# Channel norms from batch norm statistics of two interleaved groups, in place of two sums and a square

## The chip, the cores and the metric

The kernel runs on one core of a Trainium2 chip. The metric is the device time of one launch in microseconds (us). A core has a matrix engine (PE, TensorE, which writes to eight PSUM banks of 512 float32 columns), a vector engine (DVE, VectorE), an activation engine (ACT, ScalarE), a general engine (POOL, GpSimd) and a queue engine for transfers (SP). Each works through its own instruction list in order, and they wait for one another by semaphores. All data are float32.

## The reference, cut to what matters

The input `x` is an image of 128 x 128 positions with C = 32 channels. Four layers each do a convolution-like part and a feed-forward part, and each part first normalises every position over its 32 channels, eight times in all:

```python
def _ln_c(v, eps=1e-06):
    m = jnp.mean(v, axis=-1, keepdims=True)
    s = jnp.var(v, axis=-1, keepdims=True)
    return (v - m) / jnp.sqrt(s + eps)
...
    x = x + _L0_conv_ref(_ln_c(x), ...)
    t = _to_tokens(x)
    t = t + _L0_ffn_ref(_ln_t(t), ...)
    x = _from_tokens(t, x)
    ...
    x = x + _L3_conv_ref(_ln_c(x), ...)
    t = _to_tokens(x)
    t = t + _L3_ffn_ref(_ln_t(t), ...)
```

`_ln_t` is the same with eps 1e-05. What follows a norm is: a gated triangle product with a norm of its own on its output (L0, L1, L3), a mixture with pooled tokens (L0's second part), a recurrence over positions with batch statistics (L1's and L2's second part), a scan over rows with a one-dimensional convolution (L2's first part), and a mixture of eight experts (L3's second part).

## The kernel before

The whole image lies in SBUF as 128 partitions by 4096 floats, in one of two layouts, `XR` (x_rows) and `XC` (x_cols). Along a partition there are S = 32 blocks of G = 4 groups of 32 channels. The kernel is written out by hand, engine by engine: a list of stage functions for each, with semaphores between. The stages are named in the code t0, f0, t1, r1, sc, r2, t3 and f3, in the order in which they run (t: triangle product, f: feed-forward, r: recurrence, sc: scan). Each begins with a channel norm, which goes over Q = 8 chunks of four blocks (512 floats per partition, 16 groups). The helpers `ln_dve_step`, `ln_act_step` and `ln_pool_step` write out step u of this pipeline on their engine:

- DVE at step u: sum of chunk u (L279); sum of the squares of chunk u - 2 (L282); mean of chunk u (L286); reciprocal of the deviation of chunk u - 3 (L289); centring of chunk u into `Z` (L292).
- ACT at step u: root of chunk u - 2 (L301); square of chunk u (L309); copy of the transposed chunk u - 4 from PSUM to `ZT` (L318). Behind the last root it loads the table of the function that comes next (L358), where the stage names one.
- POOL at step u: for chunk u - 3 the memset of a ones channel (L330, only in t0, t1, t3 and f3), then the scaling of `Z` by the reciprocal (L333).
- PE: four transposes of a scaled chunk (L386, banks 0 and 1 in turn), then the stage's first matmuls: projections (L506) in the t stages, gate logits (L779) in f0, `Wx` (L1021) in the r stages, routing (L1376) in f3.

What surrounds the norms differs. In f0, sc and r2 nothing else is on DVE. In t0 the weights of the first stage are made among the first two steps. In t1 each of the first four steps follows four additions of f0's output (L945), whose matmuls (L838) use banks 0 to 3. In t3 each step follows an addition of r2's output (L1177). In r1 and f3 the norm is merged into the output part of the triangle stage in front (t1 and t3): a merged step t has, on DVE, gating (L674), reciprocal (L668) and sum of squares (L662) of the output part before step u = t - 5 of the norm, and on POOL a scaling of the gate (L710) and the addition to x (L715) before it:

```python
            for t in range(TRI_LN + LN_STEPS if after else S // 4 + 4):
                if 4 <= t < S // 4 + 4:
                    out_gate(t - 4)
                if 3 <= t < S // 4 + 3:
                    out_inverse(t - 3)
                if 2 <= t < S // 4 + 2:
                    out_sum(t - 2)
                if after:
                    ln_dve_step(dve, after, t - TRI_LN)
```

## Time and profile before

| | before |
|---|---|
| median of 3 runs | 674.55 us (673.01 to 675.37) |
| profiled execution, its own time | 676.27 us |
| its span | 674.5 us |
| TensorE clock granted, mean | 0.844 of full speed |
| PE busy | 486.4 us (72%) |
| DVE busy | 432.7 us (64%) |
| ACT busy | 279.9 us (42%) |
| POOL busy | 258.8 us (38%) |

The profile is one execution of the program. The span is the time from its first to its last instruction; the execution's own time has some 1.8 us more around it. Busy time counts an engine's instructions without the waits between them. A row's number is a start or a duration in us, and L279 is line 279 of the kernel. A window's row gives its bounds, its length, the busy time of PE, PE's weight loads (PEld), DVE, ACT and POOL with the number of instructions of each, the granted clock, the share of DMA and GB/s.

### The profile page before, as it was taken

How to read it: one execution, taken by the hardware profiler on the slowest of the kernel's cores; microseconds unless marked ns; L12 is line 12 of the kernel's file. 1: busy time of each engine (PE TensorE's matmuls, PEld its weight loads, DVE VectorE, ACT ScalarE, POOL GpSimd, SP SyncE). 2: the span in 40 equal slices, each digit the busy share in tenths (PEclk: the TensorE clock that was granted, in tenths of full speed). 3: DMA queues.
4: the chain of work that ended last, by engine and by line, in shares of the span. 5: the costliest groups of instructions: out<-in, count | busy, mean ns of one | idle time of the engine just before them, and what ended most of it. 6: DMA issues, size and time to landing. Idle time of an engine off the chain costs nothing.

```text
span 674.5 us, 7507 instructions
## 1 busy us (share of the span) xinstructions
PE 486.4 (72%) x2599; PEld 359.3 (53%) x2599; DVE 432.7 (64%) x845; ACT 279.9 (42%) x642; POOL 258.8 (38%) x317
## 2 busy tenths in 40 slices
PE   2788853798487674789459983799489855939992
PEld 1457742487344663389439973398246734713330
DVE  6696449532958659810873459601958497399997
ACT  2766435700375444567370006566479445000000
POOL 1793463200267237500060002300259267037774
PEclk9989976866789798889958997989579985579997
DMA  6000000000000000000000000000000000001212
GB/s 199 1 1 1 0 1 0 1 0 1 0 1 0 1 0 1 0 1 1 1 0 1 1 1 2 0 1 1 1 0 1 1 0 1 0 0 16 32 31 47
DMA packets 19572, 5.95 MB, mean 9 GB/s; under 512 B 17068, under 2 KB 19244, under 8 KB 19501
## 3 DMA queue, kind: packets, MB, share of 16 engines
q1 hardware_dynamic: 19534, 5.46, 3.6%
q8 instruction: 22, 0.36, 0.2%
q14 instruction: 16, 0.13, 0.1%
HBM read 3.36 MB, written 2.10 MB: 8 GB/s over the span
## 4 chain that ended last, share of the span: by engine, by line
PE 42%; DVE 41%; issue 6%; ACT 6%; POOL 4%; DMA 1%; DVEq 0%; SPq 0%; POOLq 0%
PE psum L1239 6%; DVE stats L279 5%; DVE gate L1456 5%; DVE ab L645 4%; PE psum L1000 4%; PE psum L999 4%; PE psum L506 4%; PE psum L536 4%; PE psum L545 4%; PE psum L386 4%; DVE stats L282 3%; DVE z L292 3%; DVE tmp L1450 3%; PE psum L1376 2%; DVE stats L286 2%
## 5 line engine op out<-in xcount | busy, mean ns | idle before, releaser
L333 POOL TENSOR_TENSOR z<-z,stats 128x496 f32<-128x496 f32 (+1 forms) x64 | 79.2, 1238 | 179.2 <-DVE stats L289 179.1
L386 PE MATMUL psum<-ident,z 128*128 128x128 f32 x256 | 58.4, 373 | 78.1 <-POOL z L333 75.5
L386 PEld LDWEIGHTS psum<-ident,z 128*128 128x128 f32 x256 | 40.8, 191 | 109.1 <-POOL z L333 75.1
L506 PE MATMUL psum<-wp_L,z_t 64*128 64x320 f32 x384 | 66.1, 479 | 11.9 <-DVE tmp L645 6.4
L1398 PE MATMUL psum<-we,z_t 128*128 128x512 f32 x128 | 64.7, 640 | 13.8 <-DVE tmp L1450 9.4
L309 ACT ACTIVATE squares<-z 128x512 f32<-128x512 f32 x64 | 40.3, 630 | 55.9 <-DVE z L292 55.9
L545 PE MATMUL psum<-wo_L,z_t 128*128 128x256 f32 x192 | 48.1, 395 | 14.6 <-DVE tmp L674 13.8
L506 PEld LDWEIGHTS psum<-wp_L,z_t 64*128 64x128 f32 x384 | 36.2, 197 | 36.6 <-issue 31.0
L1398 PEld LDWEIGHTS psum<-we,z_t 128*128 128x128 f32 x128 | 23.7, 200 | 54.0 <-DVE tmp L1450 30.1
L710 POOL TENSOR_TENSOR gate<-gate,stats 128x512 f32<-128x512 f32 x24 | 25.1, 1046 | 64.2 <-DVE stats L668 64.2
L318 ACT ACTIVATE z_t<-psum 128x512 f32<-128x512 f32 x56 | 39.8, 715 | 23.0 <-PE psum L386 22.5
L1092 ACT ACTIVATE ab<-psum,mv 128x128 f32<-128x128 f32 x112 | 41.1, 367 | 19.2 <-PE psum L1000 8.7
L1000 PE MATMUL psum<-ab,R_vt 128*128 128x128 f32 x224 | 48.4, 299 | 0.0
L1486 POOL TENSOR_TENSOR z<-tmp 128x512 f32<-128x512 f32 x31 | 39.3, 1268 | 22.9 <-DVE tmp L1450 22.9
L545 PEld LDWEIGHTS psum<-wo_L,z_t 128*128 128x128 f32 x192 | 35.4, 194 | 22.0 <-issue 16.4
L999 PE MATMUL psum<-z_t,wbnt 128*128 128x128 f32 x224 | 46.2, 290 | 0.8 <-DVE wbnt L1145 0.8
L282 DVE TENSOR_REDUCE stats<-squares 128x16 f32<-128x512 f32 x64 | 43.3, 677 | 0.0
L330 POOL MEMSET z<- 128x16 f32 x32 | 3.9, 122 | 98.7 <-ACT squares L309 98.7
L1239 PE MATMUL psum<-ab,toep 128*128 128x128 f32 x336 | 39.4, 280 | 2.5 <-POOL ab L1222 1.6
L1239 PEld LDWEIGHTS psum<-ab,toep 128*128 128x128 f32 x336 | 39.1, 195 | 3.1 <-issue 3.1
L645 DVE TENSOR_TENSOR ab<-psum,sig 128x256 f32<-128x256 f32 x64 | 33.4, 605 | 10.3 <-ACT sig L583 10.3
L1450 DVE TENSOR_TENSOR tmp<-psum,ab 128x1024 f32<-128x1024 f32 x32 | 38.8, 1214 | 0.0
(238 smaller groups left out, 1028.2 us busy)
## 6 DMA issues: line engine op xcount, KB each, us to landing
x_rows<-in_x_dram SPq DMA_DIRECT2D x4, 512.0 KB, 7.3
out_dram<-x_cols SPq DMA_DIRECT2D x32, 64.0 KB, 1.9
par<-in_par_dram SPq DMA_DIRECT2D x1, 644.5 KB
w<-in_w_dram SPq DMA_DIRECT2D x1, 264.0 KB
w<-in_w_dram SPq DMA_DIRECT2D x1, 256.0 KB
mask<-in_mask_dram SPq DMA_DIRECT2D x1, 64.0 KB
row<-in_row_dram SPq DMA_DIRECT2D x1, 3.3 KB
w2l<-in_w2l_dram SPq DMA_DIRECT2D x1, 2.0 KB
```

Of the source, the lines that this page charges most:

```text
L282: dve.tensor_reduce(SS[:, before], SQ4[:, SQ * before:SQ * (before + 1)], AX.X, ALU.add)\
L333: pool.tensor_tensor(Z4[:, r, :, 0:last_c], Z4[:, r, :, 0:last_c], rstd, ALU.mult).then_inc(L.s["z"], 1)
L386: m = pe.transpose(bank(b % 2)[:, k * N:(k + 1) * N], block_of(Z)(4 * b + k), ident[:, :])
L506: m = pe.matmul(bank(slot_bank(s) + h, 2 * 5 * C), ZT[rows, s, :], wp[l][rows, :, :], start=True, stop=True)
L545: m = pe.matmul(PSUM[:, (2 + 2 * (b % 3)) * BANK + k * 2 * GC:(2 + 2 * (b % 3)) * BANK + (k + 1) * 2 * GC], ZT[:, 4 * b + k, :], wo[l][:, ...
L645: dve.tensor_tensor(dst, slot(s)[:, :, :, 2 * C:4 * C], sig, ALU.mult).then_inc(L.s["lin"], 1)
L999: return (pe.matmul(o, W["wbnt"][:, :], chunks(ZTIME, off, h), start=True, stop=False), lambda: pe.matmul(o, W["vt"][:, :], chunks(Y, off, ...
L1000: lambda: pe.matmul(o, W["vt"][:, :], chunks(Y, off, h), start=False, stop=True))
L1092: act.activation(chunks(Y, first + k + 1, h), bank(2 * h + k % 2, NS), ACT.Sigmoid, bias=bias).then_inc(L.s[f"step_y{h}"], 1)
L1239: m = pe.matmul(bank(2 + h, ROWS_S * NB), toep[:, b, :, :], scan_rows(SCN[:, :, b:b + NB], off, h), start=(b == 0), stop=(b == 2))
L1398: m = pe.matmul(o, ZT[:, s, :], we[:, e, :, :], start=True, stop=True)
L1450: dve.tensor_tensor(TMP[:, s % 2, :].rearrange("p (e g c) -> p e g c", e=E3, g=G), PSUM[:, o:o + 2 * BANK].rearrange("p (e g c) -> p e g c ...
```

## The change

For each chunk DVE no longer takes a sum and a sum of squares of 512 elements each, and ACT no longer squares. In their place DVE issues eight `bn_stats` of 64 elements each. One reads two neighbouring groups of 32 channels alternately (channel 0 of the first group, channel 0 of the second, channel 1 of the first, ...), so that the statistics of the even elements are those of one group and the statistics of the odd ones those of the other: count, mean and sum of squared deviations of each, six numbers, into the new tile `moments`. The root is taken of the third number, and the mean is the second, so the multiplication by 1/32 (L286) goes as well.

The pipeline is ordered anew. DVE at step u: statistics of chunk u, then reciprocal and centring of chunk u - 1. ACT at step u: root of chunk u, then the copy of chunk u - 2. POOL at step u: chunk u - 1, now behind the centring instead of the square. A norm has 10 steps instead of 12. In the norms with a ones channel the centring leaves that channel out. Lastly, the output matmuls of f0 use banks 2 to 5 instead of 0 to 3, and in front of them PE waits for the weights of three more stages, whose temporary place those banks were.

```diff
         stats = sb("stats", [N, 4, N])
+        moments = sb("moments", [N, Q, SQ * G, 3])
         ident = sb("ident", [N, N])
...
-            "norm": "sum:8 mean:8 centred:8 square:8 sumsq:8 std:8 rstd:8 z:8",
+            "norm": "moments:8 std:8 rstd:8 centred:8 z:8",
...
         def ln_parts():
-            return [stats[:, k, :].rearrange("p (q s g) -> p q s g", q=Q, g=G) for k in range(4)]
+            return [stats[:, k, :].rearrange("p (q s g) -> p q s g", q=Q, g=G) for k in (0, 3)]
+
+        def ln_moment(q, k):
+
+            return moments[:, q, :, k].rearrange("p (s g) -> p s g", g=G)
...
-        LN_STEPS = Q + LAG + 2
+        LN_STEPS = Q + LAG
+
+        def last_channel(L):
+
+            return C - 1 if "one" in L.s else C
 
         def ln_dve_step(dve, L, u):
 
             X4 = by_block(L.src) if L is sc else blocks(L.src).rearrange("p g s c -> p s g c")
-            Z4, SQ4 = by_block(Z), by_block(SQR)
-            SUM, MEAN, SS, RSTD = ln_parts()
-            q, before, first = u, u - LAG, u - LAG - 1
+            Z4 = by_block(Z)
+            STD, RSTD = ln_parts()
+            q, before = u, u - 1
             if 0 <= q < Q:
                 wait_all(dve, L.ready[q])
-                r = slice(SQ * q, SQ * (q + 1))
-                dve.tensor_reduce(SUM[:, q], X4[:, r], AX.X, ALU.add).then_inc(L.s["sum"], 1)
+                for s in range(SQ):
+                    for g in range(0, G, 2):
+                        k = s * G + g
+                        m = dve.bn_stats(moments[:, q, k:k + 2, :].rearrange("p k m -> p (k m)"),
+                                         X4[:, SQ * q + s, g:g + 2, :].rearrange("p g c -> p c g"))
+                m.then_inc(L.s["moments"], 1)
             if 0 <= before < Q:
-                dve.wait_ge(L.s["square"], L.at["square"] + before + 1)
-                dve.tensor_reduce(SS[:, before], SQ4[:, SQ * before:SQ * (before + 1)], AX.X, ALU.add)\
-                    .then_inc(L.s["sumsq"], 1)
+                r, c = slice(SQ * before, SQ * u), last_channel(L)
+                dve.wait_ge(L.s["std"], L.at["std"] + before + 1)
+                dve.reciprocal(RSTD[:, before], STD[:, before]).then_inc(L.s["rstd"], 1)
+                dve.wait_ge(L.s["moments"], L.at["moments"] + before + 1)
+                dve.tensor_tensor(Z4[:, r, :, 0:c], X4[:, r, :, 0:c],
+                                  ln_moment(before, 1).unsqueeze(3).to_broadcast([N, SQ, G, c]), ALU.subtract)\
+                    .then_inc(L.s["centred"], 1)
+
+        def ln_act_step(act, L, u):
+            STD, _ = ln_parts()
+            q = u
             if 0 <= q < Q:
-                dve.wait_ge(L.s["sum"], L.at["sum"] + q + 1)
-                dve.tensor_scalar(MEAN[:, q], SUM[:, q], 1.0 / C, None, ALU.mult).then_inc(L.s["mean"], 1)
-            if 0 <= first < Q:
-                dve.wait_ge(L.s["std"], L.at["std"] + first + 1)
-                dve.reciprocal(RSTD[:, first], SUM[:, first]).then_inc(L.s["rstd"], 1)
-            if 0 <= q < Q:
-                dve.wait_ge(L.s["mean"], L.at["mean"] + q + 1)
-                dve.tensor_tensor(Z4[:, r], X4[:, r], over_c(MEAN[:, q]), ALU.subtract).then_inc(L.s["centred"], 1)
-
-        def ln_act_step(act, L, u):
-            Z4, SQ4 = by_block(Z), by_block(SQR)
-            SUM, _, SS, _ = ln_parts()
-            q = u - LAG
-            if 0 <= q < Q:
-
-                act.wait_ge(L.s["sumsq"], L.at["sumsq"] + q + 1)
-                act.activation(SUM[:, q], SS[:, q], ACT.Sqrt, bias=eps[:, L.eps:L.eps + 1],
+                act.wait_ge(L.s["moments"], L.at["moments"] + q + 1)
+                act.activation(STD[:, q], ln_moment(q, 2), ACT.Sqrt, bias=eps[:, L.eps:L.eps + 1],
                                scale=(1.0 + L.e2) / C).then_inc(L.s["std"], 1)
                 if q == Q - 1 and L.function is not None:
                     warm_table(act, L.function)
-            q = u
-            if 0 <= q < Q:
-                r = slice(SQ * q, SQ * (q + 1))
-                act.wait_ge(L.s["centred"], L.at["centred"] + q + 1)
-                act.activation(SQ4[:, r], Z4[:, r], ACT.Square).then_inc(L.s["square"], 1)
-            q = u - LAG - 2
+            q = u - LAG
             if 0 <= q < Q:
                 act.wait_ge(L.s["zt_ps"], L.at["zt_ps"] + q + 1)
                 dst = ZT[:, 4 * q:4 * q + 4, :]
@@ -318,19 +319,16 @@
                 act.activation(dst, bank(q % 2).rearrange("p (s n) -> p s n", s=4), ACT.Copy).then_inc(L.s["zt"], 1)
 
         def ln_pool_step(pool, L, u):
-            q = u - LAG - 1
+            q = u - 1
             if 0 <= q < Q:
-                Z4, r = by_block(Z), slice(SQ * q, SQ * (q + 1))
-                pool.wait_ge(L.s["square"], L.at["square"] + q + 1)
-                last_c = C
+                Z4, r, c = by_block(Z), slice(SQ * q, SQ * (q + 1)), last_channel(L)
+                pool.wait_ge(L.s["centred"], L.at["centred"] + q + 1)
                 if "one" in L.s:
-
-
-                    last_c = C - 1
-                    pool.memset(Z4[:, r, :, last_c:], 1.0).then_inc(L.s["one"], 1)
+                    pool.memset(Z4[:, r, :, c:], 1.0).then_inc(L.s["one"], 1)
                 pool.wait_ge(L.s["rstd"], L.at["rstd"] + q + 1)
-                rstd = ln_parts()[3][:, q].unsqueeze(3).to_broadcast([N, SQ, G, last_c])
-                pool.tensor_tensor(Z4[:, r, :, 0:last_c], Z4[:, r, :, 0:last_c], rstd, ALU.mult).then_inc(L.s["z"], 1)
+                _, RSTD = ln_parts()
+                pool.tensor_tensor(Z4[:, r, :, 0:c], Z4[:, r, :, 0:c],
+                                   RSTD[:, q].unsqueeze(3).to_broadcast([N, SQ, G, c]), ALU.mult).then_inc(L.s["z"], 1)
 
...
-            for V in (t1, t3):
-                pe.wait_ge(V.s["w_dve"], V.at["w_dve"] + TRI_W)
+            for V, count in ((t1, TRI_W), (t3, TRI_W), (f3, 2), (r1, 1), (r2, 1)):
+                pe.wait_ge(V.s["w_dve"], V.at["w_dve"] + count)
             for b in range(SEGI // 2):
                 if b >= 4:
                     pe.wait_ge(L.s["done"], L.at["done"] + b - 3)
                 for k in range(2):
                     i = 2 * b + k
-                    m = pe.matmul(bank(b % 4)[:, k * SEG * C:(k + 1) * SEG * C], WGT[:, i * N:(i + 1) * N],
+                    m = pe.matmul(bank(2 + b % 4)[:, k * SEG * C:(k + 1) * SEG * C], WGT[:, i * N:(i + 1) * N],
                                   outm[:, :, :], start=True, stop=True)
                 m.then_inc(L.s["y_ps"], 1)
...
                 dve.wait_ge(L.s["y_ps"], L.at["y_ps"] + b + 1)
                 for k in range(2):
                     x = xi[:, 2 * b + k]
-                    i = dve.tensor_tensor(x, x, bank(b % 4)[:, k * SEG * C:(k + 1) * SEG * C]
+                    i = dve.tensor_tensor(x, x, bank(2 + b % 4)[:, k * SEG * C:(k + 1) * SEG * C]
                                           .rearrange("p (s c) -> p s c", s=SEG), ALU.add)
```

**Order, first place.** DVE in the middle of f0's norm, before (`stats` holds sums, means, deviations and reciprocals, `squares` the squares, `z` the centred values):

```order
L279 TENSOR_REDUCE stats<-x_cols 128x16
L282 TENSOR_REDUCE stats<-squares 128x16
L286 TENSOR_SCALAR stats<-stats 128x16
L289 RECIPROCAL stats<-stats 128x16
L292 TENSOR_TENSOR z<-x_cols,stats 128x512
```

and from the start of f0's norm in the changed kernel:

```order
L290 BN_STATS moments<-x_cols 128x6 x16
L296 RECIPROCAL stats<-stats 128x16
L298 TENSOR_TENSOR z<-x_cols,moments 128x512
L290 BN_STATS moments<-x_cols 128x6 x8
L296 RECIPROCAL stats<-stats 128x16
```

Five instructions for each chunk have become ten, eight of them statistics, and the reciprocal and centring of a chunk now stand behind the statistics of the next.

**Order, second place.** DVE in one full step of r1's norm, which is merged with the output part of t1. Before:

```order
L674 TENSOR_TENSOR tmp<-psum,gate 128x512
L668 RECIPROCAL stats<-stats 128x16
L662 TENSOR_REDUCE stats<-squares 128x16
L279 TENSOR_REDUCE stats<-x_cols 128x16
L282 TENSOR_REDUCE stats<-squares 128x16
L286 TENSOR_SCALAR stats<-stats 128x16
L289 RECIPROCAL stats<-stats 128x16
L292 TENSOR_TENSOR z<-x_cols,stats 128x512
```

and in the changed kernel (its L672, L666 and L660 are the first three of these):

```order
L672 TENSOR_TENSOR tmp<-psum,gate 128x512
L666 RECIPROCAL stats<-stats 128x16
L660 TENSOR_REDUCE stats<-squares 128x16
L290 BN_STATS moments<-x_cols 128x6 x8
L296 RECIPROCAL stats<-stats 128x16
L298 TENSOR_TENSOR z<-x_cols,moments 128x512
```

The centring that stands behind a gating is now that of the chunk one step older than before.

**Order, third place.** POOL at the end of r1's norm, before:

```order
L710 TENSOR_TENSOR gate<-gate,stats 128x512
L715 TENSOR_TENSOR x_cols<-x_rows,tmp 128x4x4x32
L333 TENSOR_TENSOR z<-z,stats 128x512
L715 TENSOR_TENSOR x_cols<-x_rows,tmp 128x4x4x32
L333 TENSOR_TENSOR z<-z,stats 128x512 x5
```

and in the changed kernel (its L708, L713 and L330 are the same three):

```order
L708 TENSOR_TENSOR gate<-gate,stats 128x512
L713 TENSOR_TENSOR x_cols<-x_rows,tmp 128x4x4x32
L330 TENSOR_TENSOR z<-z,stats 128x512
L713 TENSOR_TENSOR x_cols<-x_rows,tmp 128x4x4x32
L330 TENSOR_TENSOR z<-z,stats 128x512 x3
```

Two more of the eight scalings stand among the output part's operations, and two fewer behind them.

## Rows read from the trace of the kernel before

**Rows 1.** The chain that ended last, shares of the span by engine.

```profile
PE 42%; DVE 41%; issue 6%; ACT 6%; POOL 4%; DMA 1%; DVEq 0%; SPq 0%; POOLq 0%
```

**Rows 2.** Windows, one for each norm: t0, f0, t1, r1, sc, r2, t3, f3.

```profile
5.27:29.62 24.35, 13.56 (x52) 8.63 (x52) 18.59 (x50) 11.17 (x23) 10.36 (x17) 1.00 0.32 97
104.11:123.61 19.50, 10.48 (x37) 6.20 (x38) 16.85 (x40) 11.44 (x24) 9.80 (x9) 0.65 0.00 0
169.21:193.61 24.40, 15.28 (x63) 10.13 (x61) 21.08 (x52) 11.18 (x23) 10.37 (x16) 0.69 0.00 0
249.59:280.99 31.40, 17.30 (x68) 11.00 (x67) 29.62 (x59) 17.09 (x33) 24.30 (x21) 0.84 0.00 1
332.85:352.69 19.84, 7.70 (x28) 5.01 (x28) 16.84 (x40) 13.36 (x25) 9.80 (x8) 0.54 0.00 0
408.97:428.34 19.37, 9.79 (x33) 5.62 (x34) 18.04 (x43) 12.15 (x22) 9.79 (x8) 0.74 0.00 1
472.50:495.47 22.97, 10.88 (x43) 6.81 (x41) 20.42 (x47) 11.34 (x24) 10.36 (x16) 0.54 0.00 1
539.01:570.84 31.83, 16.13 (x67) 12.20 (x65) 28.63 (x56) 15.29 (x34) 24.87 (x29) 0.72 0.00 1
```

**Rows 3.** Timeline, f0's norm: start us, us, engine, line, operation.

```profile
110.83 1.33 POOL L333 TENSOR_TENSOR z<-z,stats 128x512 f32<-128x512 f32 x1 [14.55 <-DVE stats L289]
...
114.60 0.65 DVE L292 TENSOR_TENSOR z<-x_cols,stats 128x512 f32<-128x512 f32 x1
114.83 1.33 POOL L333 TENSOR_TENSOR z<-z,stats 128x512 f32<-128x512 f32 x1 [0.66 <-DVE stats L289]
...
115.17 0.68 DVE L279 TENSOR_REDUCE stats<-x_cols 128x16 f32<-128x512 f32 x1
115.77 0.67 DVE L282 TENSOR_REDUCE stats<-squares 128x16 f32<-128x512 f32 x1
...
116.44 0.24 DVE L289 RECIPROCAL stats<-stats 128x16 f32<-128x16 f32 x1
116.60 0.65 DVE L292 TENSOR_TENSOR z<-x_cols,stats 128x512 f32<-128x512 f32 x1
...
122.14 1.28 ACT L358 ACT_TABLE_LOAD   x1
```

**Rows 4.** Timeline, r1's merged norm.

```profile
254.07 1.26 POOL L715 TENSOR_TENSOR x_cols<-x_rows,tmp 128x512 f32<-128x512 f32 x1
254.16 1.21 DVE L286 TENSOR_SCALAR stats<-stats 128x16 f32<-128x16 f32 x1
...
269.76 1.64 DVE L292 TENSOR_TENSOR z<-x_cols,stats 128x512 f32<-128x512 f32 x1
```

**Rows 5.** Groups by line: busy us, mean ns of one, idle before.

```profile
L286 DVE TENSOR_SCALAR stats<-stats 128x16 f32<-128x16 f32 x64 | 19.1, 298 | 0.6
L710 POOL TENSOR_TENSOR gate<-gate,stats 128x512 f32<-128x512 f32 x24 | 25.1, 1046 | 64.2 <-DVE stats L668 64.2
L945 DVE TENSOR_TENSOR x_cols<-x_cols,psum 128x256 f32<-128x256 f32 x16 | 5.7, 414 | 3.1 <-PE psum L838 3.1
L1456 DVE TENSOR_REDUCE gate<-z 128x128 f32<-128x512 f32 x31 | 32.1, 1034 | 0.2 <-POOL z L1486 0.2
```

**Rows 6.** Timeline, r1's batch statistics of 512 contiguous PSUM elements, five together.

```profile
279.71 3.02 DVE L1121 BATCH_NORM_STATS2 bns<-psum 128x6 f32<-128x512 f32 x5
```

**Rows 7.** Timeline, the first constants.

```profile
2.75 0.37 DVE L414 TENSOR_REDUCE d<-ident 128x32 f32<-128x128 f32 x1 [2.75 <-POOL gw L409]
3.04 0.28 DVE L415 TENSOR_REDUCE m<-ident 128x4 f32<-128x128 f32 x1
3.23 0.35 DVE L416 TENSOR_REDUCE d<-ident 128x16 f32<-128x128 f32 x1
```

**Rows 8.** Timeline, t0's third chunk, and f3's sixth scaling (chunk 5).

```profile
12.48 0.68 DVE L279 TENSOR_REDUCE stats<-x_rows 128x16 f32<-128x512 f32 x1
...
567.46 1.02 POOL L333 TENSOR_TENSOR z<-z,stats 128x496 f32<-128x496 f32 x1
```

## The prediction

> **What bounds the kernel now.** I read the chain that ended last first: PE has 42% of it and DVE 41%, and every other engine a few per cent [rows 1]. No engine is full over the whole span, so what a change is worth has to be read stage by stage. The change touches the eight channel norms, called here by the names that their stages have in the code: t0, f0, t1, r1, sc, r2, t3, f3. So I next took one window for each norm, from its first sum (L279) to the end of its last scaled chunk (L333). Added up they are 193.7 us of 674.5, and DVE is busy for 170 us of them [rows 2]. The norms are DVE's: in sc, DVE is busy 16.8 of 19.8 us while PE has 7.7.
>
> The timeline of f0's norm shows the repeating step. The centring starts at 114.60, the next chunk's sum at 115.17, the sum of squares of an older one at 115.77, the mean behind it, the reciprocal at 116.44, the next centring at 116.60: a step of 2.00 us with no gap [rows 3]. The reader should look at starts, not at durations: a reduction lasts 0.68 but the next instruction starts 0.6 after it. In starts, the step is sum 0.60, sum of squares and mean together 0.67, reciprocal 0.16, centring 0.57.
>
> There is a second thing to see, a resource that DVE and POOL hold in turn. In r1's norm POOL's addition L715 runs from 254.07 to 255.33, and the tiny mean beside it takes 1.21 us; over 64 of them the mean is 298 ns, 19.1 us in all [rows 4, 5]. The centring, with two SBUF inputs, is held as well: 1.64 us at 269.76, where that of f0 at 114.60 takes 0.65 [rows 3, 4]. It works the other way too: the scaling at 114.83 starts in the middle of a centring and takes 1.33, where one with nothing beside it takes 1.02 (567.46) [rows 3, 8]. Reductions are not held: those of 115.17 and 115.77 run at their 0.68 under that same scaling [rows 3].
>
> **The change part by part.** Removed for each chunk on DVE: sum, sum of squares, mean, in starts 116.44 - 115.17 = 1.27 us, more where the mean was held (19.1 us of means against 64 x 0.17 = 10.9: 8 us of holding, nearly all in r1 and f3). Removed on ACT: one square of 0.63 us, off the limiting engine except as latency. Added on DVE: eight batch norm statistics of 64 elements. Everything hangs on the price of one, which no row shows. The same operation on 512 elements: five in 3.02 us, each some 0.68 long, so (3.02 - 0.68) / 4 = 0.585 from start to start [rows 6]. Two reductions in order split such a slot into its parts: 0.60 for 512 elements (115.17 to 115.77 [rows 3]) and 0.19 for 128 (L415, 3.04 to 3.23 [rows 7]) give 0.41 / 384 = 1.07 ns an element and 0.05 fixed. With 64 elements that is 0.07 + 0.055 = 0.125: the lower bound, 1.0 us for the eight.
>
> But the new reads alternate between two groups, each element far from the last. The rows price this for reductions. At the kernel's start L414 reads 128 elements with a large inner step and its successor starts 0.29 later, against the 0.19 of L415, which reads the same 128 in order [rows 7]. So 0.10 / 128, about 0.75 ns for each element. L1456 reads 512 strided in 1034 ns, against 0.68 us for the 512 read in order [rows 3, 5]: 0.69 ns. For 64 elements that adds 0.045 to 0.05: **0.17 us each, 1.36 for the eight**. I take this one, since its rows share the access pattern. The upper bound is the whole duration with no overlap, fixed 0.15 + 0.11 for strided elements = 0.26.
>
> The Trainium skill speaks against the change here: "SBUF — State Buffer", section "Specifications (TRN2)", gives 16-byte lines, wants at least two hits on a line for full bandwidth, and charges every crossing to a new one. Interleaved, every read crosses. By that rule the eight cost some 1.36 and the sum below holds, 13.9 us saved; without it 1.0, and 28 saved. The trace agrees (0.29 against 0.19), though with four groups and not two.
>
> So DVE's steady step goes from 2.00 to 1.36 + 0.16 + 0.57 = 2.10: as throughput, the change loses 0.1 us a chunk. What it gains is latency. Before, chunk q was scaled three steps after its first sum (sum, centring, ACT square, sum of squares, ACT root, reciprocal). Now it is one step (statistics, ACT root, reciprocal, centring). And the mean's waits for POOL go.
>
> A new wait takes part of it back: the scaling now needs the centring just before it, and both use the held resource. In the steady part this fits (scaling 1.05 under statistics 1.36). At the end, the last centring waits for the scaling of chunk 6 and the last scaling waits for it: 0.05 + 1.05 + 0.66 + 0.05 + 1.05 = 2.9 us behind chunk 6's centring, 3.0 with the memsets of the norms that have a ones channel. Queued behind that centring on DVE is only the next stage's work.
>
> Norm by norm, after against before [rows 2]:
> - sc: 1.36 + 7 x 2.10 + 2.9 = 19.0 against 19.84; with copies behind it, 1.0 saved.
> - r2: 19.0 against 19.37; 0.5.
> - f0: 19.0 against 19.50, but the first chunk is ready at 1.36 + 2.10 + 1.1 = 4.6 instead of 110.83 + 1.33 - 104.11 = 8.05 [rows 3], 3.4 earlier, so PE no longer ends late; and ACT's table load, which stood ahead of the last copies at 122.14 [rows 3], starts near 119.8, before the last chunk. Between 0.5 and 3.4: 2.4.
> - t0: DVE goes on at 12.48 after the weights in both [rows 8]. 12.48 + 6 x 2.10 + 3.0 = 28.1 against 29.62; with the same table load 1.9.
> - t1: three of its steps have four additions of 0.41 each, overlapped 0.35 [rows 5], so 3.5 a step: 1.36 + 3 x 3.5 + 4 x 2.10 + 3.0 = 23.3 against 24.40; with the load 1.5.
> - t3: six steps have an addition of 512 elements, a slot of 0.60: 1.36 + 6 x 2.7 + 2.10 + 3.0 = 22.7 against 22.97; PE, which starts 3 us earlier and ends this stage, makes it 2.0.
> - r1 and f3 are merged with the output part of the stage before. There POOL's two operations (L710 1.05 and L715 1.26 [rows 4, 5]), centring and scaling share the resource: 1.05 + 1.26 + 0.66 + 1.05 = 4.0 a step. That is no faster than now, but the scalings start two steps sooner. f3: 539.01 + 1.4 + 5 x 4.0 + 3.1 + some 0.9 of slips = 564.4 for chunk 5, which ended at 567.46 + 1.02 = 568.48 [rows 8] and behind which PE turns it and does the routing matmuls: 3.8 saved. r1: PE is bound by the banks that the output part frees and then by its own 512-column matmuls: 0.8.
>
> Sum: 1.0 + 0.5 + 2.4 + 1.9 + 1.5 + 2.0 + 3.8 + 0.8 = **13.9 us saved**. The five further PE waits and the move to banks 2 to 5 in f0's output cost nothing: those weights are made long before, beside the pooling; without that cover they would cost the length of a weight copy, about 1 us. The profiled execution took 676.27 us (span 674.5), which is 1.7 above the median of the runs; 676.3 - 13.9 = 662.4, and against the median 674.55 - 13.9 = **660.6**.
>
> **The rivals.** (a) Interleaving costs nothing, since only two places alternate: 0.125 each, the step is 1.73. Eight chunks at 0.36 less are 2.9 us in each of the six norms that DVE bounds, of which the scaling (1.05 + 0.66 of the step) leaves some 2.4, so 14.5 more: 28 saved, **646**. For it speaks that no row has two groups; against it that L414 returns to its four places too and pays. (b) The slower side: consecutive small statistics overlap little. From 0.17 upward each 0.01 costs 0.64 us of DVE, nearly all but r1's and f3's on the path, about 0.4 in the sum, so the change turns slower from 0.17 + 0.035 = 0.205 on. At 0.22 it is +5, at 0.26 +20: **680 to 695**. Five in 3.02 us disagree [rows 6]. (c) The statistics use the shared resource, so they can't run under the scaling: each step is 1.05 longer, 48 chunks in the six norms that DVE bounds, less the 14 saved: some +36, 711. The reductions, the nearest rows, are not held. (d) The latency gained is not used, because PE or ACT end the stages anyway: 669 to 676.
>
> **How the numbers follow.** Forecast 0.55 (652 to 669), (a) 0.20 (640 to 652), (d) 0.12, (b) 0.10, (c) 0.03. The runs before lie within 0.35% of each other, so 0.3%, 2 us, is what a measurement can tell. Faster: 0.55 + 0.20 + 0.07 of (d) = 0.82. Same: the other 0.05 of (d). Slower: (b) and (c), 0.13. The range 642 to 676 leaves out (b), (c) and the low end of (a).
>
> **What would show it.** L290's eight should take 1.4 to 1.45 us as a group, some 0.26 each. f0's DVE step should be 2.10, with the first scaling's end some 3.4 us earlier and its last only 0.5. Scalings should go back to about 1.05 and a few centrings rise to 1.2 to 1.7 (the last of each norm, and most in r1 and f3). Idle time of POOL before L330 should name the centring. f3's chunk 5 should end 4 us sooner than the rest explains. The prediction is wrong if a statistic starts every 0.125 (a) or 0.2 us (b).

## The result, and the profile after

The changed kernel took 835.82 us (median of four runs, 835.27 to 836.11), the kernel before in the same session 673.96 (673.01 to 675.37): a ratio of 1.239, 95% interval 1.237 to 1.241. It is 162 us slower, where 14 us faster were predicted. The profiled execution took 836.11, its span is 834.3.

The place shows at once. Of the profile after, the chain and the groups that have grown or are new (busy us, mean ns of one, idle before):

```profile
PE 56%; DVE 30%; issue 5%; ACT 4%; POOL 4%; DVEq 0%; POOLq 0%
L1237 PE MATMUL psum<-ab,toep 128*128 (+1 forms) x1680 | 219.1, 282 | 15.4 <-DVE ab L1286 5.2
L1286 DVE SCALAR_TENSOR_TENSOR ab<-psum,gate 128x128 f32 (+1 forms) x280 | 81.8, 292 | 156.0 <-PE psum L1237 156.0
L330 POOL TENSOR_TENSOR z<-z,stats 128x496 f32<-128x496 f32 (+1 forms) x64 | 67.4, 1054 | 336.9 <-DVE z L298 336.9
L290 DVE BATCH_NORM_STATS2 moments<-x_cols 128x6 f32<-128x64 f32 x384 | 53.1, 212 | 1.5 <-POOL x_cols L713 1.1
```

The same two lines of the scan in the trace of before, two lines further down in the file:

```profile
L1239 PE MATMUL psum<-ab,toep 128*128 128x128 f32 x336 | 39.4, 280 | 2.5 <-POOL ab L1222 1.6 <-DVE tmp L1299 1.0
L1288 DVE SCALAR_TENSOR_TENSOR ab<-psum,gate 128x128 f32<-128x128 f32 x56 | 16.4, 292 | 27.9 <-PE psum L1239 27.9
```

The number to read is the count, not the time of one. A matmul takes 282 ns where it took 280; there are 1680 of them where there were 336, and 280 additions in place of 56. PE's share of the chain goes from 42% [rows 1] to 56%. The 224 further additions are 7 x 16 x 2, and the code says what has those factors. The scan of stage sc goes over 128 rows in eight pieces of 16 at once. A first pass of WARM = 12 warm-up rows guesses where each piece starts, a second pass does the 16 rows, and then the guesses are compared with what the second pass reached (the semaphores are left out here, and `...` marks further lines left out):

```python
WARM = 12
GENERAL_SCANS = ROWCH - 1           # 7
FIXED_TOL = 2.0 ** -22
...
            dve.tensor_tensor(differ.rearrange("p (k n) -> p k n", n=NB), kept, ends, ALU.subtract)
            dve.tensor_reduce(mv[:, 10:11], differ, AX.X, ALU.max, apply_absolute_value=True)
            set_flag(dve, L, bank(1)[0:1, 0:GC])
...
            with dve.If(differs != 0):
                with dve.Fori(0, GENERAL_SCANS) as r:
                    with dve.Fori(0, CHUNK // 2) as pair:
...
```

If the largest difference is above 2^-22, a general loop repeats the 16 rows seven times. That is 7 x 16 double steps; a double step is one row for each of the two streams into which the scan is split. DVE's timeline around the flag (L1113) after the change: the first additions of the loop, one at the start of a new repeat of the 16 rows, the last, and the first addition of the output:

```profile
376.13 0.14 DVE L1113 TENSOR_SCALAR flag_i<-flag_f 1x1 int32<-1x1 f32 x1
379.04 0.29 DVE L1286 SCALAR_TENSOR_TENSOR ab<-psum,gate 128x128 f32 x1 [2.77 <-PE psum L1237]
379.69 0.29 DVE L1286 SCALAR_TENSOR_TENSOR ab<-psum,gate 128x128 f32 x1 [0.36 <-PE psum L1237]
380.69 0.29 DVE L1286 SCALAR_TENSOR_TENSOR ab<-psum,gate 128x128 f32 x1 [0.70 <-PE psum L1237]
...
406.44 0.29 DVE L1286 SCALAR_TENSOR_TENSOR ab<-psum,gate 128x128 f32 x1 [1.50 <-PE psum L1237]
...
569.27 0.29 DVE L1286 SCALAR_TENSOR_TENSOR ab<-psum,gate 128x128 f32 x1 [0.38 <-PE psum L1237]
572.09 3.08 DVE L1326 TENSOR_TENSOR x_rows<-x_rows,psum 128x512 f32<-128x512 f32 x5 [2.52 <-PE psum L1231]
```

And before:

```profile
397.97 0.14 DVE L1115 TENSOR_SCALAR flag_i<-flag_f 1x1 int32<-1x1 f32 x1
399.00 3.67 DVE L1328 TENSOR_TENSOR x_rows<-x_rows,psum 128x512 f32<-128x512 f32 x6 [0.89 <-PE psum L1233]
```

From the flag's end to the output it is 572.09 - 376.27 = 195.8 us after, and 399.00 - 398.11 = 0.9 before: 194.9 us of loop. And the flag itself is set 398.11 - 376.27 = 21.8 us earlier than before. So the change pays up to there, more than was predicted for the whole, and then a branch is taken that the kernel before did not take.

The norms themselves, DVE in t0's steady part after the change:

```profile
15.25 1.11 DVE L290 BATCH_NORM_STATS2 moments<-x_rows 128x6 f32<-128x64 f32 x8
16.28 0.23 DVE L296 RECIPROCAL stats<-stats 128x16 f32<-128x16 f32 x1
16.43 0.61 DVE L298 TENSOR_TENSOR z<-x_rows,moments 128x496 f32<-128x496 f32 x1
16.96 1.11 DVE L290 BATCH_NORM_STATS2 moments<-x_rows 128x6 f32<-128x64 f32 x8
```

The step is 16.96 - 15.25 = 1.71 us, against the 2.00 of [rows 3] and the predicted 2.10. The eight statistics take 1.03 of it from start to start, 0.129 each, although a single one lasts 212 ns.

### The profile page after: what moved, and what is told of

Same layout as the page of the kernel before. It is cut to its first block, busy times and chain, and to the rows that moved or that the text cites. A ratio compares the mean times of both kernels' runs of the same rounds, so it can differ in the third digit from the quotient of the medians.

```text
span 834.3 us, 12505 instructions
## 1 busy us (share of the span) xinstructions
PE 662.4 (79%) x3959; PEld 517.4 (62%) x3959; DVE 472.1 (57%) x1389; ACT 241.7 (29%) x578; POOL 248.2 (30%) x317
## 4 chain that ended last, share of the span: by engine, by line
PE 56%; DVE 30%; issue 5%; ACT 4%; POOL 4%; DVEq 0%; POOLq 0%
PE psum L1237 26%; DVE moments L290 5%; DVE gate L1454 4%; DVE ab L643 4%; PE psum L998 4%; PE psum L997 3%; PE psum L504 3%; PE psum L543 3%; PE psum L384 3%; PE psum L534 3%; DVE z L298 3%; DVE tmp L1448 2%; PE psum L1019 2%; PE psum L1374 2%; ACT z_t L319 1%
## 5 line engine op out<-in xcount | busy, mean ns | idle before, releaser
L1237 PE MATMUL psum<-ab,toep 128*128 (+1 forms) x1680 | 219.1, 282 | 15.4 <-DVE ab L1286 5.2
L1237 PEld LDWEIGHTS psum<-ab,toep 128*128 128x128 f32 x1680 | 197.8, 190 | 36.9 <-issue 36.9
L1286 DVE SCALAR_TENSOR_TENSOR ab<-psum,gate 128x128 f32 (+1 forms) x280 | 81.8, 292 | 156.0 <-PE psum L1237 156.0
L330 POOL TENSOR_TENSOR z<-z,stats 128x496 f32<-128x496 f32 (+1 forms) x64 | 67.4, 1054 | 336.9 <-DVE z L298 336.9
L384 PE MATMUL psum<-ident,z 128*128 128x128 f32 x256 | 55.5, 359 | 47.2 <-POOL z L330 44.7
L739 ACT ACTIVATE x_cols<-psum 128x512 f32<-128x512 f32 x8 | 7.9, 1033 | 252.4 <-PE psum L728 252.4
L543 PE MATMUL psum<-wo_L,z_t 128*128 128x256 f32 x192 | 48.1, 395 | 11.9 <-DVE tmp L672 11.1
L290 DVE BATCH_NORM_STATS2 moments<-x_cols 128x6 f32<-128x64 f32 x384 | 53.1, 212 | 1.5 <-POOL x_cols L713 1.1
L708 POOL TENSOR_TENSOR gate<-gate,stats 128x512 f32<-128x512 f32 x24 | 25.1, 1047 | 52.3 <-DVE stats L666 52.2
```

Source lines behind the costliest of these rows:

```text
L290: m = dve.bn_stats(moments[:, q, k:k + 2, :].rearrange("p k m -> p (k m)"), X4[:, SQ * q + s, g:g + 2, :].rearrange("p g c -> p c g"))
L330: pool.tensor_tensor(Z4[:, r, :, 0:c], Z4[:, r, :, 0:c], RSTD[:, q].unsqueeze(3).to_broadcast([N, SQ, G, c]), ALU.mult).then_inc(L.s["z"], 1)
L384: m = pe.transpose(bank(b % 2)[:, k * N:(k + 1) * N], block_of(Z)(4 * b + k), ident[:, :])
L543: m = pe.matmul(PSUM[:, (2 + 2 * (b % 3)) * BANK + k * 2 * GC:(2 + 2 * (b % 3)) * BANK + (k + 1) * 2 * GC], ZT[:, 4 * b + k, :], wo[l][:, ...
L1237: m = pe.matmul(bank(2 + h, ROWS_S * NB), toep[:, b, :, :], scan_rows(SCN[:, :, b:b + NB], off, h), start=(b == 0), stop=(b == 2))
L1286: return dve.scalar_tensor_tensor(out=scan_rows(SCN[:, :, 1:1 + NB], off + 1, h), in0=bank(2 + h, ROWS_S * NB).rearrange("p (k n) -> p k n ...
```

## The experiments

The theory (A): the new norms round differently, this leaves the scan's two passes more than 2^-22 apart, the general loop costs 195 us, and all else is a gain of some 33. Its rivals: the extra matmuls come of changed waits or of a norm that is computed wrongly (B), or the loop is dear only in the changed kernel (C). Twelve kernels ran, four at a time beside the kernel before, whose medians were 674.64, 674.83 and 673.82.

**e1_after_loose**, the changed kernel with the scan's limit alone looser:

```diff
-        def set_flag(dve, L, differences):
+        def set_flag(dve, L, differences, tol=FIXED_TOL):
...
-            set_flag(dve, L, bank(1)[0:1, 0:GC])
+            set_flag(dve, L, bank(1)[0:1, 0:GC], 2.0 ** -18)
```

> The changed kernel with the scan's check alone made looser: its two passes may differ by 2^-18 where 2^-22 was allowed. Theory A (the lost time is the general loop of the scan, which runs because rounding now leaves the two passes more than 2^-22 apart): L1237 has 336 matmuls and L1286 56 additions again, the 195.8 us from the flag (376.27) to the first addition of the output (572.09) shrink to the 0.89 of before, and the time is 835.8 - 194.9 = 641, which would also be the change's own gain, 33 us. Rival B (the extra matmuls come of the changed waits or banks, or the two passes are far apart because the norm is computed wrongly): 1680 matmuls still, 836.

Measured: 641.63 us (five runs), ratio 0.951, 0.949 to 0.953. The group of the scan:

```profile
L1237 PE MATMUL psum<-ab,toep 128*128 128x128 f32 x336 | 39.7, 281 | 2.5 <-POOL ab L1220 1.6
```

336 matmuls, and the time that A gave. B falls. Without the loop the change is worth 33 us, 4.9%.

**e2_before_forced**, the kernel before with the limit at -1 in the same place.

> The kernel before with the scan's limit set to -1, so that the flag is always 1 and the general loop always runs, over data that it leaves as they were. Theory A: the price of the loop is 112 double steps and belongs to no part of the change, so before becomes 674 + 195 = 869, and it has 1680 matmuls in L1239. Rival C (the loop costs little where the norms are the old ones, and the changed kernel is slow in it for another reason, its clock for instance): under 800.

Measured: 869.59 us, ratio 1.289 (1.286 to 1.292), 195.0 above before:

```profile
L1239 PE MATMUL psum<-ab,toep 128*128 (+1 forms) x1680 | 218.8, 281 | 15.5 <-DVE ab L1288 5.2
```

The loop has the same price in the old kernel. C falls. 869.59 - 674.64 = 195.0 and 835.82 - 641.63 = 194.2 are the same branch, bought once by hand and once by rounding.

**e3_after_tol21** and **e4_before_tol23**: the limit doubled for the changed kernel and halved for the one before, one run each.

> The changed kernel with the scan's limit at 2^-21, twice that of before. If the two passes differ by last-bit rounding only (a value between 2 and 4 has steps of 2^-22, so two such steps are 2^-21), the loop does not run: 641. If they are further apart than two last bits, it runs: 836.

> The kernel before with the scan's limit at 2^-23, half of its own. If before stood right at the limit (its passes differ by one step of 2^-22 in at least one value of 2 or more), the loop runs: 869. If its passes had met to the last bit and the new norms break that, it does not run: 674.

Measured: 643.43 us with 336 matmuls, and 868.36 us with 1680. So the largest difference is above 2^-23 and at most 2^-22 before, above 2^-22 and at most 2^-21 after. Both readings take it that a kernel's difference is the same in every run; of after, four runs in four took the loop. Before the change the kernel stood within a factor of two of the limit, and nothing in its profile says so: a comparison that passes looks the same however narrowly it does.

**e5_in_order**, e1 with the statistics' reads in order:

```diff
-                                         X4[:, SQ * q + s, g:g + 2, :].rearrange("p g c -> p c g"))
+                                         X4[:, SQ * q + s, g:g + 2, :])
```

> As e1_after_loose (the scan's limit at 2^-18), but each batch norm statistic reads its 64 elements in order, 32 of one group and then 32 of the next, where the change alternates between the two. What it leaves out: the mean and the variance are then those of the even and of the odd channels of two groups together, not of one group each, so the output isn't the reference's. The amount read and the instructions are the same. If interleaving costs nothing (the trace of after has 0.129 us from one statistic's start to the next): 641.6 again, within 0.3%. If it has a price, as the prediction had it, the statistics now start less than 0.129 apart, and 64 x 8 of them at up to 0.04 less, most of it on the path, give 625 to 638.

Measured: 639.84 us, ratio 0.949 (0.947 to 0.951), whose interval overlaps that of e1. The same place in t0:

```profile
15.19 1.10 DVE L290 BATCH_NORM_STATS2 moments<-x_rows 128x6 f32<-128x64 f32 x8
16.20 0.24 DVE L296 RECIPROCAL stats<-stats 128x16 f32<-128x16 f32 x1
```

Eight in order have a slot of 16.20 - 15.19 = 1.01, eight interleaved 1.03 (15.25 to 16.28 above). Over the other groups of eight in these two traces the slots are nearly all 1.01 to 1.03 in order and 1.02 to 1.04 interleaved. Interleaving costs some 0.02 us in eight statistics here, where the prediction had put 0.36.

**e6_before_eps**, **e12_after_eps**: no instruction differs from before and after, only a constant of the scan's norm.

```diff
-            for k, v in enumerate((EPS_C * EPS, EPS, EPS_C)):
+            for k, v in enumerate((EPS_C * EPS, EPS, 1.02 * EPS_C)):
```

> The kernel before with the small constant of the scan's norm alone changed, 1.02e-6 for 1e-6; no instruction is added, moved or taken away, and the result moves by a part in 10^8, so only which values round up or down changes. If the branch is taken by chance of rounding and before stood right at the limit, as e4_before_tol23 showed, the loop may run: 869. If it takes what is special to the new norm, it does not: 674.

> The changed kernel with the edit of e6_before_eps: the small constant of the scan's norm 1.02e-6 for 1e-6, the limit 2^-22 and the 12 warm-up rows as they were. If whether the loop runs is the luck of the last bits, this may let it off: 641.6. If the sum of small roundings in all eight new norms puts the two passes reliably apart, it runs again: 836.

**e7_new_in_sc_only**, **e8_old_in_sc_only**: both norms in one kernel, with semaphores of their own, and the stage chooses:

```diff
+OLD_NORM = ("SC",)
...
+            if L.name in OLD_NORM:
+                return old_dve_step(dve, L, u)
```

> Batch norm statistics in the scan's own norm alone, the old norm in the seven others, the scan's limit 2^-22 as in both kernels. In e1_after_loose the stretch from the scan's first statistic to r2's is 3.3 us shorter than before. So 671 if the loop does not run, 866 if it does. That it runs would say that the rounding of the norm that feeds the scan directly is enough to trip it.

> The reverse: the old norm in the scan's alone, batch norm statistics in the seven others, the limit 2^-22. If the scan's own norm is what trips the check, the loop does not run: 641.6 + 3.3 = 645, a kernel faster than both with the check as it was. If the last bits that come from any norm ahead of it decide as well, it runs: 840.

Measured, one run each: e6 673.53, e12 642.04, e7 671.75, e8 642.68 us, all with 336 matmuls in the scan. None of the four ran the loop. The most telling is e12: the changed kernel, its limit and its warm-up untouched, is 194 us faster for 2% more of a constant of 10^-6, which moves the result by a part in 10^8 where the variance is near 1 (an estimate; no run printed the variance). So the new norm does not put the passes reliably apart; neither the scan's own norm nor the seven others do so by themselves. With 12 warm-up rows and the limit 2^-22, six kernels that differ in rounding alone as far as the scan sees them (before, after, e6, e7, e8, e12) ran the loop once in six. My expectation for e8 asked whether the scan's norm or those ahead of it decide. e7, e8 and e12 together say that neither does by itself: a change of the last bits anywhere ahead of the check can tip it. For e8 I had also expected the scan's 3.3 us back (645); 642.68 is 1 above e1, of another session, which one run can't split.

**e9_eleven_stats**, e1 with three more statistics a chunk that nothing reads:

```diff
+                for e in range(3):
+                    dve.bn_stats(extra[:, q, e, :], X4[:, SQ * q + e, 0:2, :].rearrange("p g c -> p c g"))
```

> As e1_after_loose (the scan's limit at 2^-18), with three more statistics for each chunk that nothing reads, ahead of the eight. At 0.129 from start to start the DVE step of a norm goes from 1.71 to 2.10, which is the step that the prediction assumed. It tells whether the price of a statistic was the only thing wrong in the sum of savings. If it was, this kernel saves the 13.9 us of the prediction: 674.7 - 13.9 = 661. If the shorter way from a chunk's statistics to its scaling was valued too low as well, it saves more: 650 to 657.

Measured: 663.16 us, ratio 0.983 (0.981 to 0.985). DVE in f0:

```profile
105.29 0.48 DVE L289 BATCH_NORM_STATS2 extra<-x_cols 128x6 f32<-128x64 f32 x3
105.67 1.11 DVE L293 BATCH_NORM_STATS2 moments<-x_cols 128x6 f32<-128x64 f32 x8
106.69 0.24 DVE L299 RECIPROCAL stats<-stats 128x16 f32<-128x16 f32 x1
106.84 0.64 DVE L301 TENSOR_TENSOR z<-x_cols,moments 128x512 f32<-128x512 f32 x1
107.39 0.48 DVE L289 BATCH_NORM_STATS2 extra<-x_cols 128x6 f32<-128x64 f32 x3
```

The step is 107.39 - 105.29 = 2.10, the predicted one, and 10.7 us are saved (by the interval 9.9 to 13.1) where the prediction had 13.9. So the price of the statistic was the main thing wrong in the sum, and the rest of it was, if anything, too generous. Against e1, 0.39 us more in each of 64 chunks, 24.8 on DVE, cost 663.16 - 641.63 = 21.5, or 0.87 of it. Not all of that is DVE's time on the path, as the windows under "The sum" below show.

**e10_warm14**, the changed kernel with 14 warm-up rows in the scan and the limit left at 2^-22:

```diff
+SCAN_WARM = 14
+SCAN_ROUNDS = ((CHUNK - SCAN_WARM, SCAN_WARM, 0), (0, CHUNK, SCAN_WARM))
+SCAN_STEPS = SCAN_WARM + CHUNK
```

> The changed kernel with its limit at 2^-22 as it was, but with 14 warm-up rows in the scan in place of 12. Two more double steps of 1.34 us. If the two passes are apart because 12 rows leave a remainder that still shrinks, they meet and the loop does not run: 641.6 + 2.7 = 644.3. If what is left is last-bit noise that more rows do not remove, it runs: 838.5.

Measured: 640.46 us (median of four, of which three took 640.3 to 640.5 and one 649.9), ratio 0.949, 0.947 to 0.952. The loop does not run:

```profile
L1240 PE MATMUL psum<-ab,toep 128*128 128x128 f32 x360 | 42.4, 280 | 2.5 <-POOL ab L1223 1.6
```

Two more rows of two streams are 4/56 of the scan, and 360 is 336 x 60/56; hence 3 us more in the scan (42.4 against 39.7 busy); in the whole they are not to be seen, since e1 and e10, of two sessions, differ by 1.2 us the other way. This is the version to keep: it is 5% faster than the kernel before and 23% faster than the changed one, with the check as strict as it was. By its expectation, passes that meet with 14 rows are the sign of a remainder of the guess that still shrinks; but five of six roundings passed with 12 rows too, so this one run doesn't tell a remainder from last-bit noise. How much of the difference is either stays open, and so does whether 14 rows leave more room, since no run measured how far below 2^-22 the difference now is.

**e11_banks_alone**, the kernel before with the change's edits to f0's output and nothing else:

```diff
-            for V in (t1, t3):
-                pe.wait_ge(V.s["w_dve"], V.at["w_dve"] + TRI_W)
+            for V, count in ((t1, TRI_W), (t3, TRI_W), (f3, 2), (r1, 1), (r2, 1)):
+                pe.wait_ge(V.s["w_dve"], V.at["w_dve"] + count)
...
-                    m = pe.matmul(bank(b % 4)[:, ...], ...
+                    m = pe.matmul(bank(2 + b % 4)[:, ...], ...
```

> The kernel before with the other part of the change alone: f0's output in banks 2 to 5 and the three more waits of PE in front of it, the norms left as they are. The prediction gave this no cost, since the weights are made long before: 674.7, within 0.3%. If the waits or banks matter, up to 1 us either way for each norm that they touch, 672 to 677.

Measured: 675.75 us, ratio 1.002 (1.000 to 1.004). No gain and at most 0.4% loss, and the interval touches 1. The profile shows none where the edit acts: from the start of f0's norm to that of t1's it is 168.52 - 103.50 = 65.02 us, against 169.21 - 104.11 = 65.10 before [rows 2], and from there to r1's, 248.85 - 168.52 = 80.33 against 249.59 - 169.21 = 80.38. The matmuls and waits in question run across the boundary of these two stretches.

## Why the prediction was wrong, point by point

**The step that failed** is one that the sum did not have. It took it as given that the changed kernel goes the same way through the program as the one before, and priced only the instructions that the diff adds and removes. The change alters the last bits of its results, and the program has a branch that asks about last bits. It costs 194 to 195 us (e1 against after, e2 against before), and no rival named it: all four were about what the instructions of the norms cost or gain. What could have been read beforehand is the code: a limit of 2^-22, which is one float32 step of a value between 2 and 4 (whether the scan has such values no run printed), in front of a loop of 112 double steps. That would have given a rival on the slower side, 112 times the scan's double step of 1.34 us or more, 150 upwards. Its chance could not have been read: by e4 the kernel before was within a factor of two of the limit, and of six roundings one went over.

**The price of a statistic.** 0.17 us each was predicted, 1.36 for eight; it is 0.129, 1.03 for eight. The fault lies in the rows that I priced it by: L414 [rows 7] and L1456 [rows 5] are reductions and step through four places, this one is a batch norm statistic and alternates between two, and e5 shows that this costs next to nothing (0.02 in eight). Whether the operation or the number of places makes the difference, no run separates. The bound from below, 0.125, worked out from five statistics in 3.02 us [rows 6] and two reductions, was right within some 3%, and it is rival (a), at 0.20, that held on this point. Of the signs that the prediction gave, the eight as a group last 1.11 us in place of 1.4 to 1.45, and one 0.21 in place of 0.26.

The rule of the Trainium skill that I laid beside it ("SBUF — State Buffer", "Specifications (TRN2)": every crossing to a new 16-byte line pays) is not borne out here: each read of the interleaved statistic crosses, and its slot is 1.03 against 1.01. The other rule of the Trainium skill, by which the next operation waits for an empty pipe ("VectorE: DVE Perf Modes", "The DRAIN you can't avoid"), would have made it 8 x 0.212 = 1.7 if the whole duration is the pipe's; starts 0.129 apart with 0.212 each exclude that for this operation. The same section of the Trainium skill goes on to say that an operation that isn't held starts earlier, which the prediction left out and which the trace bears out.

**The sum.** The windows of the norms in e1, from the first statistic (L290) to the end of the last scaling (L330), in the order of [rows 2]:

```profile
5.27:25.54 20.27, 13.17 (x52) 8.31 (x52) 15.91 (x90) 7.17 (x17) 8.69 (x17) 1.00 0.38 114
99.31:115.09 15.78, 10.10 (x40) 5.63 (x40) 13.87 (x80) 7.39 (x17) 8.81 (x9) 0.78 0.00 0
159.34:179.59 20.25, 12.91 (x61) 8.33 (x59) 18.63 (x92) 7.38 (x17) 8.68 (x16) 0.83 0.00 0
234.69:264.98 30.29, 16.93 (x68) 11.35 (x67) 25.38 (x99) 11.54 (x25) 23.12 (x21) 0.83 0.00 1
316.97:332.93 15.96, 7.80 (x28) 5.00 (x28) 14.76 (x80) 9.12 (x17) 8.38 (x8) 0.55 0.00 1
389.77:406.01 16.24, 9.88 (x33) 5.84 (x34) 15.59 (x82) 7.66 (x14) 8.38 (x8) 0.79 0.00 1
450.10:469.33 19.23, 12.68 (x51) 7.88 (x49) 17.33 (x87) 7.62 (x17) 9.04 (x16) 0.56 0.00 1
510.25:539.10 28.85, 15.88 (x70) 12.54 (x69) 24.71 (x96) 11.13 (x27) 23.74 (x29) 0.73 0.00 1
```

The same windows in e9, whose step is the predicted one:

```profile
5.28:27.58 22.30, 14.01 (x52) 8.81 (x52) 18.55 (x114) 7.58 (x17) 9.06 (x17) 1.00 0.36 104
101.78:120.62 18.84, 11.32 (x40) 6.21 (x40) 16.93 (x104) 7.74 (x17) 8.82 (x9) 0.73 0.00 0
164.99:188.04 23.05, 14.42 (x61) 9.24 (x59) 21.05 (x116) 7.46 (x17) 9.04 (x16) 0.78 0.00 1
243.94:274.78 30.84, 16.79 (x68) 11.34 (x67) 26.84 (x123) 11.66 (x25) 23.28 (x21) 0.83 0.00 1
326.72:345.55 18.83, 7.64 (x28) 5.00 (x28) 16.91 (x104) 9.79 (x16) 8.83 (x8) 0.54 0.00 0
402.60:420.44 17.84, 9.44 (x33) 5.39 (x34) 17.84 (x106) 8.57 (x14) 7.81 (x8) 0.80 0.00 0
466.45:488.73 22.28, 13.22 (x51) 8.17 (x49) 20.38 (x111) 7.63 (x17) 9.05 (x16) 0.54 0.01 1
531.85:560.09 28.24, 14.58 (x72) 11.75 (x71) 25.78 (x120) 11.14 (x27) 23.84 (x29) 0.82 0.00 1
```

Both sets have the columns of a window's row. Subtracted from [rows 2], and below it the saving of the whole stretch, from one norm's start to the next one's (f3's to the end of the span, 642.0 and 662.6 against 674.5):

| | t0 | f0 | t1 | r1 | sc | r2 | t3 | f3 | sum |
|---|---|---|---|---|---|---|---|---|---|
| predicted | 1.9 | 2.4 | 1.5 | 0.8 | 1.0 | 0.5 | 2.0 | 3.8 | 13.9 |
| the norm's window, e1 | 4.1 | 3.7 | 4.2 | 1.1 | 3.9 | 3.1 | 3.7 | 3.0 | 26.8 |
| norm to norm, e1 | 4.8 | 5.1 | 5.0 | 1.0 | 3.3 | 3.2 | 6.4 | 3.7 | 32.5 |
| norm to norm, e9 | 2.3 | 1.9 | 1.4 | 0.5 | 0.2 | -0.3 | 1.1 | 4.7 | 11.9 |

At the price that the prediction assumed (e9), each of its terms is within 1 us and their sum is 2.0 above what was measured. For the small ones that is no confirmation: sc and r2 were to save 1.0 and 0.5 and saved 0.2 and nothing. At the true price (e1) the windows of the six norms that DVE bounds each give 1.3 to 2.9 us more than predicted, as rival (a) had it (2.4 each); r1 and f3, where the resource that DVE and POOL hold in turn sets the step, are as predicted within 0.2 from norm to norm.

Rival (a) gave 646 and e1 took 641.6. It put 14.5 us of sum on 64 x 0.36 = 23 us of DVE, 0.63 of it. In the windows that held: e1's add up to 166.9 us and e9's to 182.2, so 15.4 of the 24.8 us on DVE show there, 0.62. The other 5.2 us between the two kernels lie behind the norms, where their instructions are the same. They differ most behind t3's norm, from its end to the start of f3's; e1 first, then e9:

```profile
469.33:510.25 40.92, 36.58 (x252) 27.64 (x252) 25.86 (x45) 29.98 (x85) 23.80 (x20) 1.00 0.00 1
488.73:531.85 43.12, 39.14 (x252) 29.04 (x252) 26.05 (x46) 30.04 (x85) 23.88 (x20) 0.92 0.00 1
```

The same 252 matmuls keep PE busy for 36.58 us at a granted clock of 1.00 and for 39.14 at 0.92, and the stretch is 2.2 us longer. Behind r2's norm it is 0.92 against 0.89, and 1.9 us. So part of the 21.5 us goes with the clock that PE was granted and not with DVE. In the kernel before, the stretch behind t3's norm took 43.5 us at 0.97, with 8 more matmuls left to do; the 2.6 us against e1 are what t3's 6.4 has beyond its window. How the savings of e1 behind the norms, 5.7 us in all, divide between the clock and an earlier start of PE is not shown, nor why the clock differs. The clock also differs from profile to profile: f0's norm begins at 99.31 in e1 and at 96.83 in the profile of after, in the same instructions, and from 30 to 40 us the clock is 0.91 in the one and 1.00 in the other.

**The latency**: f0's first scaled chunk was to be ready 3.4 earlier, at 4.6 us. In e1 its scaling ends at 102.22 + 1.05 - 99.31 = 3.96, against 8.05:

```profile
102.22 1.05 POOL L330 TENSOR_TENSOR z<-z,stats 128x512 f32<-128x512 f32 x1 [9.98 <-DVE z L298]
103.94 1.05 POOL L330 TENSOR_TENSOR z<-z,stats 128x512 f32<-128x512 f32 x1 [0.67 <-DVE z L298]
...
112.56 2.53 POOL L330 TENSOR_TENSOR z<-z,stats 128x512 f32<-128x512 f32 x2 [0.68 <-DVE z L298]
```

That is 4.1 us earlier, 3.4 as forecast and the rest by the cheaper statistics. The last scaling ends at 115.09, 15.78 after the norm's start in place of 19.50: 3.7 earlier, where the prediction had 0.5. The scaling is at 1.05 again, and POOL's idle time names the centring (L298), as said.

**The held resource.** In the merged stages the centring was to rise to 1.2 to 1.7 and a POOL step to be 4.0. In r1 of e1:

```profile
243.42 1.05 POOL L330 TENSOR_TENSOR z<-z,stats 128x512 f32<-128x512 f32 x1 [0.63 <-DVE z L298]
244.43 1.05 POOL L708 TENSOR_TENSOR gate<-gate,stats 128x512 f32<-128x512 f32 x1
245.43 1.27 POOL L713 TENSOR_TENSOR x_cols<-x_rows,tmp 128x512 f32<-128x512 f32 x1
247.32 1.05 POOL L330 TENSOR_TENSOR z<-z,stats 128x512 f32<-128x512 f32 x1 [0.63 <-DVE z L298]
```

247.32 - 243.42 = 3.90. The centring beside it:

```profile
245.74 1.50 DVE L298 TENSOR_TENSOR z<-x_cols,moments 128x512 f32<-128x512 f32 x1
```

1.50 us. f3's chunk 5, which was to be scaled by 564.4 - 539.0 = 25.4 us after the norm's start, ends at 534.92 + 1.02 - 510.25 = 25.7, against 29.5 before [rows 2, 8]:

```profile
534.92 1.02 POOL L330 TENSOR_TENSOR z<-z,stats 128x496 f32<-128x496 f32 x1
```

So here the prediction was right in mechanism and size, although the statistics cost less than it assumed: POOL's operations and the centring set the step. (Its own figures give 568.48 - 564.4 = 4.1 saved for f3 where it put 3.8.) Rival (c), that the statistics use this resource too, is out: L290 keeps its 212 ns as a mean of 384, and in r1's and f3's windows its 64 have medians of 210 and 208.

**The slower side.** (b) put the point where the change stops paying at 0.205 for a statistic. The prediction's "each 0.01 costs 0.64 us of DVE, about 0.4 in the sum" holds for 0.001, not for 0.01 (64 x 8 of them are 0.51 us of DVE); the points 0.205, 680 and 695 were worked out with the right size. e9 gives 21.5 us for 0.048 us a statistic, 0.44 for each 0.001, the clock's part included. (d), that the latency gained is not used, is out by e1's 33 us.

**The waits and banks** are three new waits, not the five that the prediction counted, and they cost nothing that the profile of e11 shows.

## What to carry to other kernels

Ask of every change whether it moves last bits, and whether the program anywhere compares such bits: a tolerance, a speculative pass with a check, a search that ends when nothing moves. If it does, the branch behind the comparison is a rival with its full price, however small the change, and how close the old kernel stands to the limit has to be measured, since its profile does not tell: force the branch once for its price, and halve and double the limit for the margin. Compare counts of instructions before times of one: 1680 against 336 settles in one row where the time went.

For prices, take the row with the same operation and the same number of places that the reads alternate between, and where none has both, keep the unstrided bound as a case of equal weight.

Where two kernels differ behind the changed instructions as well, look at the granted clock of those stretches before putting the whole difference down to the change.

## What the runs showed of the hardware

- Batch norm statistics of 64 float32 last 0.21 us (means of 210 to 212 ns) and start 0.129 us apart. Alternating between two groups on every element costs next to nothing: 1.03 against 1.01 us for eight (e1 and e5).
- Inside the dynamic loop (its body holds two double steps, and PE and DVE wait against register values) a double step takes 380.69 - 379.04 = 1.65 us, where the straight-line scan takes two additions 0.67 apart, 1.34. The idle time before the first stream's addition is 0.70 in place of 0.38, that before the second's is 0.38 as outside. Why only the first's waits longer is not shown. At each of the six starts of a new repeat it is 1.50 to 1.54 in place of 0.70 (406.44), and the loop's first addition starts 2.77 us after the flag.
- The same 252 matmul records took PE 36.58 us at a granted clock of 1.00 and 39.14 at 0.92 (e1 and e9, behind t3's norm).
